# Two attentions rewritten as fp32 products on row tiles of TensorE, with block-diagonal keys, in a one-core transformer kernel

## The chip, the cores and the metric

The kernel runs on one core of one Trainium2 chip. The metric is the time of one execution on the device, in microseconds (us). The kernel before took 394.37 us, the median of three executions (393.59 to 395.58).

## What is computed

1024 rows (16 batches of 64) of 256 features pass through two layers, each with a cross attention and a feed-forward part:

```python
x = x + L0_xattn(layernorm(x), ctx, ctx)      # 32 query heads, 8 key/value heads, 8 features per head
x = x + L0_ffn(layernorm(x))                  # 2 experts 256 -> 1024 -> 256, the better one per row
x = x + L1_xattn(layernorm(x), ctx, Wq, Wkv_expand, Wout)   # 16 heads of 16 features, causal mask
x = x + L1_ffn(layernorm(x))                  # down to 128, 8 experts (top 2 per row) and a shared one, up to 256, plus gelu(x) @ core_w
```

An attention is softmax(q k^T * scale) v within one batch: 64 queries, 64 keys, per head.

## The kernel before

The rows lie in 8 tiles of 128 rows (2 batches each), the feed-forward parts work on 4 groups of two tiles. A tile t goes through the steps of `attn0`, its group through `ffn0`, then `attn1` and `ffn1`. `steps_and_needs` lists the steps and what each needs, `make_orders` is a list scheduler at build time that turns a table of costs (`COST`) and of preferences (`URGENCY`) into one fixed order per engine, and each engine runs its list with semaphores. PSUM has eight banks: four in ring S (attentions and small products), two in H (hidden values of the feed-forward parts), two in Y (their results). A step that fills a bank first claims it, which waits until the bank's former content has been read out.

The names, by step of a tile:

- `attn0`. POOL (`keys0`) and DVE (`queries0`) split fp32 keys and queries into three bfloat16 parts, laid out as 48 of 64 columns (`KS`, `QS`). PE transposes them (`turn_keys0`, `turn_queries0`, against `identb`), ACT and DVE copy them out (`QT`, `K2`). `scores0` multiplies them in bfloat16, four times per tile. DVE takes the row maxima and subtracts them (`scores_less_max0`: `MN`, `PT`), ACT takes the exponential, PE transposes the fp32 probabilities (`turn_probs0`, against `identf`), ACT copies them out, `values0` multiplies by the values `V2`, `turn_back` transposes, DVE divides and adds to `X`.
- `attn1`. `keys_values1` and `project` make keys, values and queries. Both are split into bfloat16 parts (`KQS`), transposed (`turn_heads1`) and copied out (`KT1`, `QT1`). `scores1` gives the scores (causal mask `maskS` by a product with `identb`), DVE takes the maxima (`largest1`), `shifts1` and `turn_shifts1` bring the negated maxima across (`MS1`, `MT1`), and `probs1` forms the transposed scores anew with the shift added by a product with `sel`, so that ACT's exponential is at once the transposed probabilities. `values1` multiplies by the values.
- `ffn0` and `ffn1`: `up0` (H<-XT,WF), `down0` (Y<-WP,A), `up1` (H<-GH,W), `down1` (Y<-A,W), with XN the normalized rows and XT their transposes. `zero_row` (S<-GB,W) works out once what each expert gives for a zero input, one column at a time.

In the trace an fp32 product stands as two records of TensorE, each with a weight load of its own; a bfloat16 product or an fp32 transpose stands as one.

## Time and profile before

| | |
|---|---|
| median of three executions | 394.37 us |
| span of the profiled execution, first to last instruction (its own time; the page has no other) | 397.0 us |
| TensorE busy, records | 366.7 us, 3768 |
| DVE / ACT / POOL busy | 234.5 / 197.6 / 91.7 us |
| granted TensorE clock, mean | 0.957 |
| bytes moved | 12.16 MB, nearly all in the first 40 us |

A record of TensorE lasts some 0.2 to 0.4 us but the next starts before it ends. What a product costs in a dense stream is therefore the distance from its start to the next start, and it is read here from the starts of consecutive groups in the timeline. Granted clock 1.00 is 2.4 GHz, 0.5 is 1.2 GHz.

### The profile page before, as it was taken

What the parts mean: (1) busy time and instruction counts of PE and PEld (TensorE: products, weight loads), DVE (VectorE), ACT (ScalarE), POOL (GpSimd) and SP (SyncE); (2) the same over time, 40 slices, a digit from 0 to 9 for tenths busy, and PEclk for the clock granted to TensorE, in tenths of its full rate; (3) what the DMA queues carried; (4) which work ended last, traced back from release to release, by engine and by line L of the source; (5) the groups of instructions that cost most, each with busy time, mean ns of one, the idle gap of its engine ahead of it and who ended that gap; (6) DMA issues with size and microseconds to landing.
All of it is one profiled execution on the core that took longest, in us unless ns stands there. A gap on an engine that the chain in (4) does not pass through costs nothing.

```text
span 397.0 us, 9308 instructions
## 1 busy us (share of the span) xinstructions
PE 366.7 (92%) x3768; PEld 305.9 (77%) x3768; DVE 234.5 (59%) x611; ACT 197.6 (50%) x403; POOL 91.7 (23%) x173
## 2 busy tenths in 40 slices
PE   1777899999999999999998999999899999997896
PEld 1466888888988888878886877878778787785783
DVE  6689668889997247302399013873756556427134
ACT  1666337567656424232343133656745665666452
POOL 7882113241123223202540312410004000200000
PEclk9988559999999999999999989999989999999899
DMA  9991000000000000000000000000000000000000
GB/s 188 415 390 72 2 1 2 0 3 2 2 0 2 2 0 2 2 3 1 2 2 2 1 3 0 2 2 0 4 28 2 0 2 30 2 1 3 25 0 27
DMA packets 8218, 12.16 MB, mean 31 GB/s; under 512 B 4464, under 2 KB 6768, under 8 KB 7408
## 3 DMA queue, kind: packets, MB, share of 16 engines
q1 hardware_dynamic: 8176, 11.57, 8.7%
q8 instruction: 30, 0.49, 0.5%
q14 instruction: 12, 0.10, 0.1%
HBM read 10.52 MB, written 1.05 MB: 29 GB/s over the span
## 4 chain that ended last, share of the span: by engine, by line
PE 85%; DVE 9%; issue 3%; ACT 2%; POOL 1%; DVEq 0%; POOLq 0%
PE Y L1252 26%; PE H L1252 24%; PE S L1252 20%; PE S L1293 4%; PE S L1353 3%; PE S L1260 2%; PE S L1317 2%; PE S L1269 1%; PE S L1418 1%; DVE PT L1016 1%; DVE MN L1015 1%; PE S L1326 1%; DVE K L1229 0%; DVE KQS L1075 0%; ACT YS L821 0%
## 5 line engine op out<-in xcount | busy, mean ns | idle before, releaser
L1252 PE MATMUL H<-XT,WF 128*128 128x256 f32 x256 | 64.3, 399 | 0.0
L1252 PE MATMUL Y<-WP,A 128*128 128x256 f32 x256 | 59.7, 381 | 0.0
L895 POOL TENSOR_TENSOR A<-R 128x512 f32<-128x512 f32 x32 | 33.4, 1043 | 98.5 <-ACT R L775 96.6
L1252 PEld LDWEIGHTS H<-XT,WF 128*128 128x128 f32 x256 | 49.0, 199 | 8.1 <-ACT R L775 0.8
L1252 PEld LDWEIGHTS Y<-WP,A 128*128 128x128 f32 x256 | 47.5, 190 | 6.0 <-issue 0.2
L803 ACT ACTIVATE A<-H,B 128x256 f32<-128x256 f32 x84 | 35.5, 473 | 28.5 <-PE H L1252 27.0
L775 ACT ACTIVATE R<-H 128x512 f32<-128x512 f32 x32 | 19.1, 597 | 58.5 <-PE H L1252 52.4
L1252 PE MATMUL Y<-A,W 128*128 128x256 f32 x168 | 45.9, 386 | 0.8 <-DVE YG L1206 0.8
L1252 PE MATMUL H<-GH,W 128*128 128x256 f32 x168 | 45.1, 396 | 0.4 <-ACT GH L792 0.4
L1206 DVE TENSOR_TENSOR YG<-YS,Y 128x256 f32<-128x256 f32 x32 | 13.5, 420 | 39.6 <-ACT YS L821 39.2
L1252 PEld LDWEIGHTS H<-GH,W 128*128 128x128 f32 x168 | 31.6, 197 | 6.1 <-issue 1.3
L1252 PEld LDWEIGHTS Y<-A,W 128*128 128x128 f32 x168 | 29.7, 191 | 6.9 <-issue 1.2
L698 ACT COPY QT<-S 128x1024 bf16<-128x1024 bf16 (+1 forms) x24 | 20.3, 885 | 15.0 <-PE S L1260 9.5
L698 ACT COPY QT_OT<-S 96x1024 bf16<-96x1024 bf16 (+1 forms) x32 | 21.0, 692 | 10.7 <-PE S L1252 6.8
L848 POOL TENSOR_TENSOR rstdf<-varef,mhalf 128x2 f32<-128x2 f32 x8 | 5.6, 699 | 89.8 <-DVE varef L971 89.7
L742 ACT ACTIVATE PT<-PT 128x512 f32<-128x512 f32 x32 | 19.6, 629 | 9.0 <-DVE PT L1016 8.9
L1293 PE MATMUL S<-identf,PT 128*128 128x128 f32 x128 | 19.6, 298 | 4.6 <-issue 2.0
L1293 PEld LDWEIGHTS S<-identf,PT 128*128 128x128 f32 x128 | 16.4, 155 | 7.5 <-issue 5.2
L698 ACT COPY PT<-S 128x512 f32<-128x512 f32 x32 | 17.6, 588 | 8.9 <-PE S L1293 8.9
L1089 DVE RECIPROCAL rec<-S 128x16 f32<-128x16 f32 x8 | 2.0, 256 | 33.1 <-PE S L1317 33.0
L821 ACT ACTIVATE YS<-Y,Y0n 128x256 f32<-128x256 f32 x32 | 15.0, 473 | 9.0 <-PE Y L1252 8.5
L1252 PE MATMUL S<-PT,V 64*32 64x64 f32 (+1 forms) x768 | 17.0, 238 | 2.5 <-issue 2.4
(189 smaller groups left out, 659.9 us busy)
## 6 DMA issues: line engine op xcount, KB each, us to landing
W<-in_w SPq DMA_DIRECT2D x2, 1344.0 KB, 11.4
WF<-in_wf SPq DMA_DIRECT2D x2, 1024.0 KB, 7.5
WP<-in_wp SPq DMA_DIRECT2D x2, 1024.0 KB, 9.6
X<-in_x SPq DMA_DIRECT2D x8, 128.0 KB, 8.2
out_dram<-X SPq DMA_DIRECT2D x8, 128.0 KB, 1.7
CD<-in_ctx_in SPq DMA_DIRECT2D x2, 256.0 KB, 5.3
C<-in_ctx_in SPq DMA_DIRECT2D x1, 256.0 KB, 3.0
CT<-in_ctxT SPq DMA_DIRECT2D x1, 256.0 KB, 4.0
```

The source lines that it names most:

```text
L698: nc.scalar.copy(dst(n, i), src(b, i)).then_inc(done, 1)
L742: nc.scalar.activation(e, e, ACT.Exp, scale=HD0 ** -0.5).then_inc(exp_ready, 1)
L775: nc.scalar.activation(R0[:, n % 2, :], b[:, :], ACT.Prelu, alpha=0.5).then_inc(done, 1)
L803: ins = nc.scalar.activation(A1[:, n % 4, :], b[:, k * GT:(k + 1) * GT], ACT.Gelu, bias=B1[:, ch:ch + 1])
L821: nc.scalar.activation(YS[:, j % 2, :], b[:, 0:GT], ACT.Identity, bias=Y0n[:, e:e + 1]).then_inc(ys_ready, 1)
L895: nc.gpsimd.tensor_tensor(flat(A0[:, n % 2, :, :]), R0[:, n % 2, :], R0[:, n % 2, :], ALU.mult).then_inc(a0_ready, 1)
L1206: nc.vector.tensor_tensor(YG[:, j % 2, :], YS[:, j % 2, :], b[:, GT:2 * GT], ALU.mult).then_inc(free["Y", "dve"], 1)
L1252: return nc.tensor.matmul(o, a, b, start=start, stop=stop, skip_group_check=shared)
L1260: ins = nc.tensor.transpose(b[:, :].bitcast(bf16)[:, p * P:(p + 1) * P], flat(QS[:, t % 2, 2 * pair_:2 * pair_ + 2, :]), identb[:, :])
L1293: ins = nc.tensor.transpose(b[:, i * P:(i + 1) * P], PT[:, t % 2, 4 * c + i, :], identf[:, :])
L1317: ins = nc.tensor.transpose(b[:, i * P:(i + 1) * P], o, identf[:, :])
L1353: ins = nc.tensor.transpose(b[:, :].bitcast(bf16)[0:96, h * P:(h + 1) * P], flat(src[:, t % 2, 8 * i + h, :, :]), identb[:, :])
```

## The change

Both attentions are now computed from fp32 queries and keys without the split.

- Keys. A tile's keys are laid out with their features on partitions (`KR0`, loaded so by DMA for layer 0; a product for layer 1) and multiplied by a 0/1 column (`quarter0`, `quarter_`) into four copies, in each of which only one head of a group of four is non-zero (`KZ0` by POOL, `KT1` by DVE). A product of the turned queries (`QT0`, `QT1`, two fp32 transposes or the product itself) with such a block gives the scores of four heads at once.
- `scores0` and `probs0` use 32 rows of the array per product, and each of the four row strips writes a PSUM bank of its own; `scores1`, `probs1` and the layer-0 shift use 64 rows. `values0` and `values1` alternate between two row halves and two banks.
- Layer 0 takes its probabilities as layer 1 did: maxima (`largest0`), turned shifts (`shifts0`, `turn_shifts0`), then a second, transposed score product with the shift added (`probs0`), and the exponential straight from PSUM. `turn_probs0`, the exponential in SBUF and its copy are gone. Layer 1's mask of the transposed scores is now in further rows of `sel` and `MT1`.
- POOL adds the result of layer 0 to `X` (`add_result0`) in DVE's place, and no longer splits keys.
- `zero_rows`: 20 fp32 products whose weights are 8 columns and whose moving side is 128 columns, in place of 20 with 128 and 1.
- `COST`, `URGENCY` (a number per step and tile), `SWITCH`, `CHANGE` and `SLACK` are new, so all orders are new. One line: `"attn0": "c 400.1 -352.5  v -755.8 129.1 ..."` became `"attn0": "c -426 -336 468 727 -863 -12 576 173; v 48 181 ..."`.

```diff
+    if part in ("attn0", "attn1") and stage in "spo":
+        return stages(part, n, {"s": f"h*{SCORE_BANKS[part]}", "p": f"f*{SCORE_BANKS[part]}", "o": "u*2"}[stage])
...
             def keys0(t, _):
                 if t == 0:
-                    pool.wait_ge(ld_c, 16)
+                    pool.wait_ge(places_ready, 1)
...
-                nc.gpsimd.tensor_scalar(KQS[:, t % 2, :, 4, :], rest, 1.0, 0.0, ALU.mult, ALU.add)
-                nc.gpsimd.tensor_tensor(KQS[:, t % 2, :, 2, :], rest, KQS[:, t % 2, :, 1, :], ALU.subtract
-                                        ).then_inc(ks1_ready, 1)
+                    filled(pool, "attn0", t - 2, "f", 3)
+                for c in range(DC):
+                    nc.gpsimd.tensor_tensor(KZ0[:, t % 2, c, :, :], KR0[:, c, t * P:(t + 1) * P].unsqueeze(1).to_broadcast([P, 4, P]),
+                                            quarter0[:, :].unsqueeze(2).to_broadcast([P, 4, P]), ALU.mult).then_inc(kz_ready, 1)
+            def add_result0(t, _):
+                read_out(pool, "attn0", t, "n", 0)
+                for half in range(2):
+                    xh = X[:, t, half * P:(half + 1) * P].rearrange("p (k g r) -> p g k r", k=4, g=2)
+                    o = O0[:, t % 2, half * P:(half + 1) * P].rearrange("p (g k r) -> p g k r", k=4, g=2)
+                    nc.gpsimd.tensor_tensor(xh, xh, o, ALU.add).then_inc(x0_ready, 1)
             def biases(g, _):
...
             def queries0(t, _):
                 wait_rstd("attn0", t)
-                link(normed("attn0", t, 0, t, Q[:, t % 2, :]))
...
-                    filled(dve, "attn0", t - 2, "q", 1)
-                q = Q[:, t % 2, :].rearrange("p (h d) -> p h d", d=HD0)
-                rest = QR[:, t % 2, :].rearrange("p (h d) -> p h d", d=HD0)
-                s = QS[:, t % 2, :, 0:SLOTS * HD0].rearrange("p h (s d) -> p h s d", d=HD0)
-                link(nc.vector.tensor_copy(s[:, :, 0:3, :], q.unsqueeze(2).to_broadcast([P, NH0, 3, HD0])))
-                link(nc.vector.tensor_tensor(rest, q, s[:, :, 0, :], ALU.subtract))
-                link(nc.vector.tensor_copy(s[:, :, 3:5, :], rest.unsqueeze(2).to_broadcast([P, NH0, 2, HD0])))
-                nc.vector.tensor_tensor(s[:, :, 5, :], rest, s[:, :, 3, :], ALU.subtract).then_inc(qs_ready, 1)
-            def blocks0(t, _):
-                b, done = filled(dve, "attn0", t, "k", 0)
-                for half in range(2):
...
+            def largest0(t, c):
+                b, done = filled(dve, "attn0", t, "h", c)
+                nc.vector.tensor_reduce(MN[:, slot("attn0", t), 8 * c:8 * c + 8],
+                                        b[:, :].rearrange("p (h t) -> p h t", t=S), AX.X, ALU.max, negate=True
+                                        ).then_inc(done, 1)
...
             def keys1(t, _):
                 b, done = filled(dve, "attn1", t, "kv", 0)
-                dve.wait_ge(kh_ready, 4 * t + 4)
+                dve.wait_ge(kh_ready, t + 1)
                 if t >= 2:
-                    dve.wait_ge(ks1_ready, t - 1)
-                nc.vector.tensor_tensor(R1[:, t % 2, :].rearrange("p (h d) -> p h d", d=HD1),
-                                        b[:, 0:D].rearrange("p (h d) -> p h d", d=HD1), KQS[:, t % 2, :, 0, :],
-                                        ALU.subtract).then_inc(done, 1)
+                    filled(dve, "attn1", t - 2, "f", 1)
+                nc.vector.tensor_tensor(KT1[:, t % 2, :, :, :].rearrange("p b c k -> p b (c k)"),
+                                        b[:, 0:D].unsqueeze(1).to_broadcast([P, 4, D]),
+                                        quarter_[:, :].unsqueeze(2).to_broadcast([P, 4, D]), ALU.mult).then_inc(done, 1)
             def rows1(t, _):
...
-            def scores0(t, c):
-                b, done = claim(pe, "attn0", t, "s", c)
-                if c == 0:
-                    read_out(pe, "attn0", t, "k", 0)
-                read_out(pe, "attn0", t, "q", c // 2)
-                for i in range(4):
-                    pair_ = 4 * c + i
-                    for bt in range(2):
-                        ins = mm(b[bt * S:(bt + 1) * S, i * P:(i + 1) * P], QT[:, t % 2, pair_, bt * S:(bt + 1) * S],
-                                 flat(K2[:, t % 2, pair_ // 2, bt, :, :]))
-                ins.then_inc(done, 1)
...
+            def scores0(t, _):
+                claims_ = [claim(pe, "attn0", t, "h", i) for i in range(4)]
+                read_out(pe, "attn0", t, "q", 0)
+                pe.wait_ge(kz_ready, 2 * t + 2)
+                for c in range(DC):
+                    for i, (b, done) in enumerate(claims_):
+                        quarter = slice(32 * i, 32 * i + 32)
+                        for bt in range(2):
+                            rows = slice(bt * S, (bt + 1) * S)
+                            ins = mm(b[rows, 4 * c * S:4 * (c + 1) * S], QT0[quarter, t % 2, c, rows], KZ0[quarter, t % 2, c, :, rows])
+                        if c == DC - 1:
+                            ins.then_inc(done, 1)
+            def turn_shifts0(t, _):
+                b, done = claim(pe, "attn0", t, "m", 0)
+                pe.wait_ge(ms0_ready, t + 1)
+                nc.tensor.transpose(b[:, :].bitcast(bf16)[:, 0:P], MS0[:, t % 2, :, :, :].rearrange("p a k h -> p (a k h)"),
+                                    identb[:, :]).then_inc(done, 1)
+            def probs0(t, _):
+                claims_ = [claim(pe, "attn0", t, "f", i) for i in range(4)]
+                read_out(pe, "attn0", t, "m", 0)
+                if t == 0:
+                    pe.wait_ge(sel0_ready, 1)
+                for j in range(8):
+                    for k in range(2):
+                        for r in range(2):
+                            i = 2 * r + k
+                            half = slice(r * S, (r + 1) * S)
+                            for bt in range(2):
+                                rows = slice(bt * S, (bt + 1) * S)
+                                mm(claims_[i][0][rows, j * S:(j + 1) * S], sel0[half, 8 * i + j, :], MT0[half, t % 2, rows],
+                                   start=(j == 0), stop=False, shared=True)
+                for j in range(8):
+                    c, r = divmod(j, 4)
+                    for i, (b, done) in enumerate(claims_):
+                        quarter = slice(32 * i, 32 * i + 32)
+                        for bt in range(2):
+                            rows = slice(bt * S, (bt + 1) * S)
+                            ins = mm(b[rows, j * S:(j + 1) * S], KZ0[quarter, t % 2, c, r, rows], QT0[quarter, t % 2, c, rows],
+                                     start=False, shared=True)
+                        if j == 7:
+                            ins.then_inc(done, 1)
...
             def values0(t, _):
-                b, done = claim(pe, "attn0", t, "o", 0)
+                claims_ = [claim(pe, "attn0", t, "u", bt) for bt in range(2)]
                 pe.wait_ge(v2_ready, 2 * t + 2)
-                read_out(pe, "attn0", t, "p", 3)
-                o = b[:, :].rearrange("p (h g b s) -> p h g b s", h=2, g=2, b=2)
+                read_out(pe, "attn0", t, "f", 3)
                 for kh in range(2):
-                    for bt in range(2):
+                    for part in range(2):
                         for k4 in range(4):
-                            kv = 4 * kh + k4
-                            ins = mm(o[32 * k4:32 * k4 + 32, kh, :, bt, :], flat(V2[:, t % 2, bt, kv, :, :]),
-                                     PT[:, t % 2, 2 * kv:2 * kv + 2, bt * S:(bt + 1) * S])
-                ins.then_inc(done, 1)
+                            first = 8 * k4 + 4 * kh + part
+                            for bt, (b, done) in enumerate(claims_):
+                                rows = slice(bt * S, (bt + 1) * S)
+                                ins = mm(b[32 * k4:32 * k4 + 32, kh * P:(kh + 1) * P], V2[rows, t % 2, 4 * kh + k4, part, :],
+                                         PT[rows, t % 2, first:first + 3:2, :], start=(kh == part == 0), stop=(part == 1), shared=True)
...
+            def scores1(t, _):
+                banks = [claim(pe, "attn1", t, "h", r)[0] for r in range(2)]
+                read_out(pe, "attn1", t, "kv", 0)
+                read_out(pe, "attn1", t, "w", 0)
+                if t == 0:
+                    pe.wait_ge(masks_ready, 3)
+                for b in banks:
                     for bt in range(2):
                         rows = slice(bt * S, (bt + 1) * S)
-                        ins = mm(b[rows, h * S:(h + 1) * S], QT1[:, t % 2, 8 * c + h, rows], KT1[:, t % 2, 8 * c + h, rows],
-                                 start=False, shared=True)
-                ins.then_inc(done, 1)
+                        mm(b[rows, :], identb[:, rows], maskS[:, :].unsqueeze(1).to_broadcast([P, 8, S]), stop=False, shared=True)
+                for c in range(DC):
+                    for r, b in enumerate(banks):
+                        half = slice(r * S, (r + 1) * S)
+                        for bt in range(2):
+                            rows = slice(bt * S, (bt + 1) * S)
+                            ins = mm(b[rows, 4 * c * S:4 * (c + 1) * S], QT1[half, t % 2, c, rows], KT1[half, t % 2, :, c, rows],
+                                     start=False, shared=True)
+                        if c == DC - 1:
+                            ins.then_inc(full["S"], 1)
...
+            def probs1(t, _):
+                banks = [claim(pe, "attn1", t, "f", r)[0] for r in range(2)]
+                read_out(pe, "attn1", t, "m", 0)
+                for j in range(8):
+                    for r, b in enumerate(banks):
+                        for bt in range(2):
+                            rows = slice(bt * S, (bt + 1) * S)
+                            mm(b[rows, j * S:(j + 1) * S], sel[:, 8 * r + j, :], MT1[:, t % 2, rows], start=(j == 0), stop=False,
+                               shared=True)
+                for j in range(8):
+                    c, k = divmod(j, 4)
+                    for r, b in enumerate(banks):
+                        half = slice(r * S, (r + 1) * S)
+                        for bt in range(2):
+                            rows = slice(bt * S, (bt + 1) * S)
+                            ins = mm(b[rows, j * S:(j + 1) * S], KT1[half, t % 2, k, c, rows], QT1[half, t % 2, c, rows],
+                                     start=False, shared=True)
+                        if j == 7:
+                            ins.then_inc(full["S"], 1)
...
+            def values1(t, _):
+                claims_ = [claim(pe, "attn1", t, "u", bt) for bt in range(2)]
+                read_out(pe, "attn1", t, "f", 1)
                 for hq in range(4):
                     for h4 in range(4):
                         h = 4 * hq + h4
-                        ins = mm(b[32 * h4:32 * h4 + 32, hq * S:(hq + 1) * S], V1[rows, t % 2, h, :], PT1[rows, t % 2, h, :])
-                ins.then_inc(done, 1)
+                        place = 8 * (hq % 2) + 4 * (hq // 2) + h4
+                        for bt, (b, done) in enumerate(claims_):
+                            rows = slice(bt * S, (bt + 1) * S)
+                            ins = mm(b[32 * h4:32 * h4 + 32, hq * S:(hq + 1) * S], V1[rows, t % 2, h, :], PT1[rows, t % 2, place, :])
+                            if h == NH1 - 1:
+                                ins.then_inc(done, 1)
             def turn_rows(part):
                 def f(g, _):
...
+            def zero_rows(g, _):
+                b, done = claim(pe, "ffn1", g, "z", 0)
+                pe.wait_ge(ld_w2, 16)
+                pe.wait_ge(gb8_ready, 1)
+                for ch in range(NCH1 - 1):
+                    ins = mm(b[0:E1, 0:L], GB8[:, ch, :], W2[:, ch, :], start=(ch == 0), stop=(ch == NCH1 - 2))
                 ins.then_inc(done, 1)
```

The order of TensorE at the start of the program, last rows up to the first product of a feed-forward part (H<-XT,WF); before:

```order
L1260 MATMUL S<-identb,QS 128x128 x16
L1252 MATMUL S<-GB,W 128x1 x13
L1418 MATMUL S<-identf,XN 128x128 x4
L1252 MATMUL S<-GB,W 128x1 x7
L1252 MATMUL S<-WR,XT 128x2 x4
L1252 MATMUL S<-K,QT 64x128 x16
L1252 MATMUL H<-XT,WF 128x256 x4
```

and after:

```order
L1243 MATMUL S<-QT,KZ 64x64 x64
L1269 MATMUL S<-identb,MS 128x128
L1243 MATMUL S<-MT,sel 64x64 x64
L1243 MATMUL S<-QT,KZ 64x64 x64
L1243 MATMUL S<-PT,V 32x128 x64
L1321 MATMUL S<-identf,OT 128x128 x4
L1249 MATMUL S<-identf,Q 128x128 x4
L1321 MATMUL S<-identf,OT 128x128 x4
L1243 MATMUL S<-KZ,QT 64x256 x16
L1429 MATMUL S<-identf,XN 128x128 x4
L1243 MATMUL S<-WR,XT 128x2 x4
L1243 MATMUL H<-XT,WF 128x256 x4
```

The split transposes (QS, KS, KQS) and half of the PT transposes that stood ahead of this place are gone; in their stead stand the shift and score products of two tiles (MT,sel and QT,KZ) and the zero-input rows have moved behind it.

TensorE at the transposed scores and the values of layer 1 for tiles 0 and 1, before:

```order
L1252 MATMUL S<-maskT,identb 64x512 x2
L1252 MATMUL S<-MT,sel 64x64 x16
L1252 MATMUL S<-QT_OT,KT 64x64 x16
L1252 MATMUL Y<-WP,A 128x256 x8
L1252 MATMUL S<-maskT,identb 64x512 x2
L1252 MATMUL S<-MT,sel 64x64 x16
L1252 MATMUL S<-QT_OT,KT 64x64 x16
```

and after (MT,sel and QT,KT are one step for all 16 heads of a tile now):

```order
L1243 MATMUL S<-MT,sel 64x64 x32
L1243 MATMUL S<-QT,KT 64x64 x32
L1243 MATMUL S<-MT,sel 64x64 x32
L1243 MATMUL S<-QT,KT 64x64 x32
L1321 MATMUL S<-identf,OT 128x128 x4
L1243 MATMUL H<-XT,WF 128x256 x4
L1243 MATMUL S<-PT,V 32x64 x64
L1243 MATMUL Y<-WP,A 128x256 x4
```

The mask product is gone, a tile's 64 products follow one another, and a feed-forward block stands between them and the values.

## Rows read from the trace of the kernel before

**Rows 1.** The page: span, busy time, slices and the chain.

```profile
span 397.0 us, 9308 instructions
...
PE 366.7 (92%) x3768; PEld 305.9 (77%) x3768; DVE 234.5 (59%) x611; ACT 197.6 (50%) x403; POOL 91.7 (23%) x173
...
PEclk9988559999999999999999989999989999999899
...
PE 85%; DVE 9%; issue 3%; ACT 2%; POOL 1%; DVEq 0%; POOLq 0%
```

**Rows 2.** Busy time of each engine in two stretches.

```profile
0.00:54.90 54.90, 38.65 (x385) 32.86 (x385) 41.03 (x96) 25.27 (x46) 29.42 (x82) 0.81 0.58 193
54.90:397.00 342.10, 328.06 (x3386) 273.05 (x3384) 193.50 (x516) 172.38 (x357) 62.30 (x91) 0.98 0.02 5
```

**Rows 3.** TensorE's timeline: start us, length, group, its records.

```profile
8.04 1.06 PE L1269 MATMUL S<-identb,KS 128*64 128x128 bf16 x16 [8.04 <-POOL KS L869]
...
54.88 3.48 PE L1252 MATMUL H<-XT,WF 128*128 128x256 f32 x8
```

**Rows 4.** TensorE's timeline through steps of layer-0 attention.

```profile
105.11 1.51 PE L1293 MATMUL S<-identf,PT 128*128 128x128 f32 x12
106.46 1.06 PE L1260 MATMUL S<-identb,QS 128*128 128x128 bf16 x16
107.44 0.64 PE L1269 MATMUL S<-identb,KS 128*64 128x128 bf16 x16
108.01 1.08 PE L1252 MATMUL S<-PT,V 128*32 128x128 f32 x32
109.02 0.41 PE L1252 MATMUL S<-K,QT 128*64 128x128 bf16 x8
109.37 2.00 PE L1252 MATMUL H<-XT,WF 128*128 128x256 f32 x8
```

**Rows 5.** TensorE's timeline through steps of layer-1 attention.

```profile
304.80 1.06 PE L1353 MATMUL S<-identb,KQS 128*96 128x128 bf16 x16
305.69 0.65 PE L1252 MATMUL Y<-A,W 128*128 128x256 f32 x2
...
326.77 0.41 PE L1252 MATMUL S<-maskT,identb 128*64 128x512 bf16 x2
327.02 0.42 PE L1252 MATMUL S<-MT,sel 128*64 128x64 bf16 x16
327.26 0.42 PE L1252 MATMUL S<-QT_OT,KT 96*64 96x64 bf16 x16
327.52 0.39 PE L1252 MATMUL S<-maskT,identb 128*64 128x512 bf16 x2
...
334.83 0.99 PE L1252 MATMUL S<-PT,V 64*32 64x64 f32 x64
335.76 0.29 PE L1468 MATMUL S<-identb,GS 128*128 128x128 bf16 x2
```

**Rows 6.** TensorE's timeline of 334.83 to 334.86 us alone.

```profile
334.83 0.26 PE L1252 MATMUL S<-PT,V 64*32 64x64 f32 x4
```

**Rows 7.** TensorE's timeline behind a burst, and the instruction DMA of 228.5 to 229 us.

```profile
228.74 1.51 PE L1252 MATMUL S<-PT,V 64*32 64x64 f32 x101
231.18 0.63 PE L1252 MATMUL S<-PT,V 64*32 64x64 f32 x27 [0.92 <-issue]
...
232.44 3.37 PE L1252 MATMUL H<-XT,WF 128*128 128x256 f32 x8
...
q8 instruction: 1, 0.02, 13.5%
```

**Rows 8.** Groups of instructions by line: busy us, mean ns, idle before.

```profile
L1022 DVE TENSOR_REDUCE MN<-S 128x8 f32<-128x512 f32 x16 | 10.4, 686 | 4.5 <-PE S L1252 4.4
L746 ACT ACTIVATE PT<-S 128x512 f32<-128x512 f32 x16 | 9.3, 596 | 11.1 <-PE S L1252 10.2
L895 POOL TENSOR_TENSOR A<-R 128x512 f32<-128x512 f32 x32 | 33.4, 1043 | 98.5 <-ACT R L775 96.6
```

525 lines of the change are left out of this document (225 added, 300 removed), and 33 rows, old and new, of the table URGENCY.

## The prediction, made before the changed kernel had run

> **What bounds the kernel now.** I read the page first. TensorE is busy for 366.7 of 397.0 us and the chain that ended last runs through it for 85% of the span [rows 1]. The other engines are busy for 59%, 50% and 23%. Then the two stretches: behind the first feed-forward product TensorE is busy for 328.1 of 342.1 us at a granted clock of 0.98. Ahead of it, 54.9 us pass with 38.7 us of records at 0.81 [rows 2]. That product starts at 54.88 us, the first record of all at 8.04 [rows 3]. So there are two accounts: the dense stream, where every us of TensorE's work counts, and the start, where the first tiles run through all engines one after the other.
>
> **Prices in the dense stream**, from start to start. An fp32 transpose of 128 columns: 12 in 1.35 us, 0.1125 us each. I take that as the price of an fp32 record by itself: 0.1125 us per 128 moving columns. On column tiles records overlap: 32 records of 128 columns on 32-wide tiles took 1.01 us in place of 3.6 [rows 4], and 64 records of 64 columns took 0.93 us in place of 3.6 [rows 5], so four tiles give close to four times. No row shows two different row strips of the array at work. I take it that they overlap like the columns, which makes the price of a record alone over the number of tiles in use (8 in layer 0 and in both value steps, 4 in layer 1's scores). Its bounds are that (full overlap) and the price on columns alone (none).
>
> **Layer 0, a tile.** Removed or replaced: 16 PT transposes 1.80 us, 16 QS 0.98, 16 KS 0.57, values 1.01, 32 score products at 8 in 0.35 us 1.4 [rows 4]. That is 5.76 us, of which the score figure holds a mode switch too often (some 0.2), so 5.56. Added: 2 transposes 0.23. Scores, 16 products, 32 records of 256 columns: 32 x 0.225 / 8 = 0.90. Shift transpose 0.06. Shift products, 64 in bfloat16 of 64 columns: those of before go at 16 in 0.24 us on two column tiles [rows 5], 15 ns each, so 0.48 on four tiles and 0.96 on two; I take 0.70. Transposed scores, 128 records of 64 columns: 128 x 0.056 / 8 = 0.90. Values, 64 records of 128 columns on 8 tiles: 0.90. Three mode switches more, about 0.1 each, 0.3. Sum 4.0. Saved: 1.55 us a tile, 12.4 us in all.
>
> **Layer 1, a tile.** Removed or replaced: 32 KQS transposes at 16 in 0.89 us, 1.78. Two score steps at 0.26, 0.52 (their mask stays). Two transposed steps of 0.25 mask, 0.24 shift and 0.26 scores, 1.50. Values 0.93 [rows 5]. Sum 4.73. Added: scores, 16 records of 256 columns on 4 tiles, 16 x 0.225 / 4 = 0.90. Shift, 32 at 15 ns, 0.48. Transposed scores, 64 x 0.056 / 4 = 0.90. Values 64 x 0.056 / 8 = 0.45. Two switches 0.2. Sum 2.93. The query and key projections stream as many columns as before: nothing. Saved 1.8 us a tile, 14.4 us in all. The zero-input rows cost 40 records either way (between -4 and +1 us, taken as nothing). **Dense account: 27 us less.** The product counts of the new order give 5105 records against 3768.
>
> **The start.** Ahead of the first feed-forward product the order of before has some 24 us of work at the dense prices, the new one 12.7 (8 fp32 transposes, scores of three tiles, two key products, shift, transposed scores and values of two tiles, 8 transposes back, XN and the router). So 31 of the 54.9 us were loss. The new chain: first queries at 6 us, POOL's key blocks two passes of 1.04 us a tile [rows 8], so scores at 7 to 8.7 on the slow clock. Then 4 maxima of 0.69, shift 0.4, transposed scores 3 us with their supply stall, 4 exponentials of 0.60 [rows 8], and the second tile behind the same banks until 24.5. Values, turn back, division, POOL's addition, layer norm and router take until about 34. Bounds 28 and 44. Loss 21 in place of 31: **10 us less**.
>
> **What hides the rest.** DVE loses four subtraction passes a tile, the key-block copies and all splits, and gains two passes' length for `KT1` (a 512-column pass is 0.69 us, so 1.4). ACT loses the copies of the transposes. POOL gains two passes of 1.04 and some 0.9 us of addition a tile and loses its ten split instructions [rows 8]. At 59%, 50% and 23% before [rows 1] none of them comes near TensorE's load, and the feed-forward blocks of 3.5 us are the cover: if they did not stand between scores and maxima, a tile of layer 0 would show 2.7 + 0.7 us of DVE and ACT, and then 2.4 us of exponentials.
>
> **Instruction supply.** Behind a burst of small records TensorE stood still for 0.92 us with nothing to wait for, after 101 of 128 value records. An instruction block of 0.02 MB was fetched at that time [rows 7]. 0.02 MB is 256 instructions, 128 records with their loads. Stepping back 128 records from the restart at 231.18 leads to 228.3, so a block can't be used up faster than in 2.9 us. I walked both orders in blocks of 128 records at the dense prices. Before, three or four places are faster than that (0.5 to 1.3 us each, 3.7 in all). After, with 192 records per transposed layer-0 step, eight places behind the start are, up to 2.0 us each, 11.7 in all. **8 us more**, between 0 and 14. The Trainium skill ("Runtime: NRT & Kernel Launch", section "Instruction fetch mechanics") says that the sequencer fetches the next page while it executes the current one and that crossing a boundary is mostly hidden. By that the sum would be 8 us lower. The 0.92 us of this trace says otherwise.
>
> **Clock.** Behind that stall 8 feed-forward records took 3.37 us against 2.00 [rows 4, 7], as they do at the lower of the two levels (1.2 and 2.4 GHz); such stretches are the 8s in the page's clock row [rows 1]. More stalls may bring two or three more such stretches of 1.4 us each: 3 more, between 0 and 14.
>
> **Sum.** 397.0 - 27 - 10 + 8 + 3 = 371 us of span. The median of before is 2.6 us below the profiled span, so I predict **368 us**.
>
> **Rivals.**
> 1. Row strips don't overlap (the slower side). Then only columns do, and layer 0's scores and transposed scores cost 3.6 us each in place of 0.9 per tile at two column tiles, shifts 0.96, values 1.8. That is 6.6 more a tile, 52 in all. Layer 1's scores, transposed scores and values are 0.9, 0.9 and 0.45 dearer, 18 in all. With the supply stall gone (-8), 368 + 62 = 430 us. It decides from the point where overlap between strips falls under about half: +26 us makes it slower than before. For it: no row shows an overlap of strips. Against it: column tiles overlap fully in fp32, and each strip has its own bank. Chance 0.11. The Trainium skill ("TensorE: Matmul & The Clock Gate", section "Measured speedup vs the span model") gives 3.07 times for four row tiles and 10.6 for sixteen, which would make this rival unlikely. No row here shows it.
> 2. A record has a least distance. The smallest mean distance of rows 5 is 15 ns, and the new steps ask for 7. If 15 held, 1024 + 1024 + 768 + 512 small records would take 3328 x 0.015 = 50 us in place of the 33 above: 385 us. Against it: four value records started inside 30 ns [rows 6]. Chance 0.10. The skill's same page (section "Wait — 56ns, not 53.3ns?") puts the least start-to-start distance at about 25 ns. By that the sum would be 50 us higher, near 418. Rows 5 and 6 contradict it, and of the 0.10 I give it 0.02.
> 3. Four banks at once. A layer-0 score or probability step claims all of ring S. If TensorE finds no feed-forward work meanwhile, 3.4 + 2.4 us a tile lie bare: 46 us for all eight, 23 for half, about 391, no change. Before, TensorE hardly waited behind the start [rows 2]. Chance 0.08.
> 4. The supply and the clock cost nothing, and the start ends at 28: 368 - 8 - 3 - 6 = 351. Chance 0.10.
>
> The forecast itself, 358 to 380, has 0.61.
>
> **Range and chances.** Rivals 2 and 4 and the forecast lie between 350 and 392, with part of rival 3: 8 in 10. Under 0.5% (2 us) a difference can't be told from none. Faster 0.83, same 0.04 (a strip overlap or bank waits that just eat the gain), slower 0.13 (rival 1, and the worse part of 3).
>
> **What the profile after would show.** Right: layer-0 score groups of 64x256 products, 32 records within a us; QT,KZ with 128 records in 0.9 to 1.2 us apart from stalls; stalls put down to issue of up to 2 us in the steps MT,sel, QT,KZ or PT,V; first H<-XT,WF near 34 us; DVE's busy time down to about 165 us, TensorE's share of the chain above 85%. Wrong: 32 score records over 3 us (strips in turn); QT,KZ evenly 15 ns apart; TensorE waiting for DVE's maxima or ACT's exponentials in mid-program; granted clock under 0.93.

## The result, and the profile after

The changed kernel takes 390.31 us (median of 7; 387.58 to 392.79) against 394.37 (median of 7). The ratio is 0.989, with a 95% interval of 0.9856 to 0.9925. It is faster by about 1%, where 7% (368 us) was forecast, and 390 lies just inside the upper end of the range. The profiled execution has a span of 387.8 us; 371 was forecast.

The page after. Its rows answer to [rows 1]:

```profile
span 387.8 us, 11733 instructions
...
PE 345.8 (89%) x5105; PEld 282.2 (73%) x5105; DVE 163.6 (42%) x481; ACT 150.4 (39%) x349; POOL 90.8 (23%) x134
...
PEclk9999969989999999899999999999999999999899
...
PE 82%; issue 6%; DVE 4%; SPq 3%; ACT 3%; POOL 1%; DMA 1%; DVEq 0%; POOLq 0%
```

TensorE has 5105 records, as counted, and 21 us less busy time. But the chain now holds two names that it lacked before, SPq (SP issuing DMAs, 3%) and DMA (1%), and twice the share of issue. The two stretches, cut at the new place of the first feed-forward product, answer to [rows 2]:

```profile
0.00:53.20 53.20, 26.00 (x650) 19.43 (x651) 22.79 (x57) 12.90 (x31) 26.61 (x54) 0.96 0.60 209
53.20:388.00 334.80, 319.79 (x4456) 262.75 (x4456) 140.84 (x424) 137.48 (x318) 64.23 (x80) 0.98 0.02 5
```

This settles where to look. Behind the first feed-forward product the forecast was 371 - 34 = 337 us; it took 334.6 (387.8 - 53.23), against 342.1 before. The start was to fall from 54.88 to 34 us and fell to 53.23: **19 us late, a little more than the whole miss**. Inside those 53 us TensorE's records fell from 38.7 to 26.0 us, so its work shrank as forecast, and waiting took its place: TensorE stood for 27.2 us. The clock of 0.96 can't be set beside the 0.81 of [rows 2]. The profile counts a stretch for which it has no clock record as full speed, and its first record here lies at 42.55 us (at 16.97 in the kernel before, so that 0.81 is too high as well). Steps ahead of it take up to twice their later time (tile 0's scores 1.94 us against 1.05), as they would at the lower level. TensorE's timeline through the start (start, length, group, idle before it and what ended it; of the scores of tiles 0 and 1, which stand in groups of 4 records, only the first group):

```profile
7.69 0.70 PE L1243 MATMUL H<-KZ,QT 32*64 32x256 f32 x4 [1.99 <-POOL KZ L882]
...
16.94 1.22 PE L1243 MATMUL S<-CT,WKV 64*128 64x128 f32 x4 [6.62 <-DMA WKV<-in_wkv]
...
23.54 1.07 PE L1243 MATMUL S<-MT,sel 64*64 64x64 bf16 x64 [0.66 <-ACT MT L718]
24.54 1.51 PE L1243 MATMUL S<-QT,KZ 32*64 32x64 f32 x74
29.91 1.21 PE L1243 MATMUL S<-QT,KZ 32*64 32x64 f32 x54 [3.86 <-issue]
...
36.18 2.20 PE L1243 MATMUL S<-QT,KZ 32*64 32x64 f32 x121 [1.28 <-issue]
39.42 0.65 PE L1243 MATMUL S<-PT,V 64*32 64x128 f32 x6 [1.04 <-ACT PT L766]
...
53.23 3.22 PE L1243 MATMUL H<-XT,WF 128*128 128x256 f32 x7
```

Two things strike. TensorE stands 6.62 us for layer 1's key and value weights, which its order has ahead of tile 1's scores and the shift of tile 0. And the first burst of short records stands 3.86 us for nothing but its own instructions; the longest such stall of before was 2.0 us. SP's queue says why the weights are late (issue time, length, count):

```profile
1.18 2.67 SPq L679 DMA_DIRECT2D KR<-in_ctxT  x4
...
4.51 2.53 SPq L679 DMA_DIRECT2D KR<-in_ctxT  x4
...
8.81 2.55 SPq L679 DMA_DIRECT2D KR<-in_ctxT  x4
11.41 0.60 SPq L689 DMA_DIRECT2D CT<-in_ctxT  x1
12.05 0.60 SPq L690 DMA_DIRECT2D WKV<-in_wkv  x1
```

An issue costs SP some 0.6 us here, for 32 KB (KR, the first eight) as for 256 KB (CT), and the replicated keys are 12 issues, 7.75 us. In the kernel before WKV was issued at 2.83 us.

### The profile page after: what moved, and what is told of

It reads as the page before. It is cut to its first block, busy times and chain, and to the rows that moved or that the text cites. A ratio compares the mean times of both kernels' runs of the same rounds, so it can differ in the third digit from the quotient of the medians.

```text
span 387.8 us, 11733 instructions
## 1 busy us (share of the span) xinstructions
PE 345.8 (89%) x5105; PEld 282.2 (73%) x5105; DVE 163.6 (42%) x481; ACT 150.4 (39%) x349; POOL 90.8 (23%) x134
## 3 DMA queue, kind: packets, MB, share of 16 engines
HBM read 11.04 MB, written 1.05 MB: 31 GB/s over the span
## 4 chain that ended last, share of the span: by engine, by line
PE 82%; issue 6%; DVE 4%; SPq 3%; ACT 3%; POOL 1%; DMA 1%; DVEq 0%; POOLq 0%
PE Y L1243 27%; PE S L1243 27%; PE H L1243 24%; SPq L679 2%; PE S L1321 2%; DMA WKV<-in_wkv 1%; ACT PT L766 1%; PE S L1429 1%; PE S L1330 1%; POOL X L891 1%; SPq L674 1%; DVE XN L1002 0%; DVE MN L1030 0%; ACT YS L842 0%; PE S L1249 0%
## 5 line engine op out<-in xcount | busy, mean ns | idle before, releaser
L1243 PE MATMUL Y<-WP,A 128*128 128x256 f32 x256 | 64.0, 399 | 0.0
L1243 PE MATMUL H<-XT,WF 128*128 128x256 f32 x256 | 62.1, 391 | 0.0
L1243 PEld LDWEIGHTS Y<-WP,A 128*128 128x128 f32 x256 | 48.9, 199 | 8.1 <-issue 1.5
L1243 PEld LDWEIGHTS H<-XT,WF 128*128 128x128 f32 x256 | 47.9, 194 | 7.9 <-issue 1.5
L766 ACT ACTIVATE PT<-S 128x512 f32<-128x512 f32 x32 | 16.7, 602 | 30.1 <-PE S L1243 30.1
L1243 PE MATMUL S<-QT,KZ 32*64 32x64 f32 x1024 | 15.8, 255 | 10.2 <-issue 10.2
L882 POOL TENSOR_TENSOR KZ<-KR,quarter 128x512 f32<-128x512 f32 x16 | 16.3, 1039 | 33.8 <-PE S L1243 32.0
L1243 PEld LDWEIGHTS S<-QT,KZ 32*64 32x64 f32 x1024 | 13.8, 149 | 11.3 <-issue 10.9
L1046 DVE TENSOR_REDUCE MN<-S 128x8 f32<-128x512 f32 x16 | 10.4, 685 | 22.5 <-PE S L1243 22.5
L1014 DVE TENSOR_SCALAR Q<-X,mv,rstd 128x256 f32<-128x256 f32 x8 | 4.1, 516 | 34.2 <-POOL rstd L869 15.8
L1030 DVE TENSOR_REDUCE MN<-S 128x8 f32<-128x512 f32 x24 | 15.1, 680 | 6.6 <-PE S L1243 6.6
```

The lines of the kernel that those rows point to most:

```text
L766: nc.scalar.activation(flat(PT[:, t % 2, 8 * c:8 * c + 8, :]), b[:, :], ACT.Exp, scale=HD0 ** -0.5).then_inc(done, 1)
L882: nc.gpsimd.tensor_tensor(KZ0[:, t % 2, c, :, :], KR0[:, c, t * P:(t + 1) * P].unsqueeze(1).to_broadcast([P, 4, P]), quarter0[:, :].unsque ...
L1030: nc.vector.tensor_reduce(MN[:, slot("attn0", t), 8 * c:8 * c + 8], b[:, :].rearrange("p (h t) -> p h t", t=S), AX.X, ALU.max, negate=True ...
L1046: nc.vector.tensor_reduce(MN[:, slot("attn1", t), 8 * c:8 * c + 8], b[:, :].rearrange("p (h t) -> p h t", t=S), AX.X, ALU.max, negate=True ...
L1243: return nc.tensor.matmul(o, a, b, start=start, stop=stop, skip_group_check=shared)
```

## Experiments

Theory 1: SP's queue makes the start late. Theory 2: the instruction supply sets it. Theory 3: the chain through DVE and ACT sets it. Theory 4 came after the first runs: the supply is slow because data loads fill the DMA engines. Ratios are to the kernel before, which ran again beside each group of runs (medians 394.4 to 395.9 us), each with its 95% interval. The changed kernel stands at 0.989 (0.986 to 0.993), with its first feed-forward product at 53.23 us. "First product" means that one from here on; times inside a run are from its one trace.

### Three ways to have WKV early

WKV first:

```diff
             keys(0, 0, 1)
+            sp.dma_start(CT[:, :], ctxT).then_inc(ld_kv, 16)
+            sp.dma_start(WKV1[:, :], wkv1).then_inc(ld_kv, 16)
             rows(1)
```

> The two loads that layer 1's key and value step needs (CT, WKV) are issued behind the first tile's rows and keys, 12 issues earlier; nothing else changes. Theory 1 (SP's queue of issues makes the start late): WKV is issued near 4.5 us in place of 12.05 and has landed near 9.5, so the wait of 6.62 us for it goes, the first feed-forward product comes 5 to 7 us earlier than 53.23, and the time falls by 5 to 7 us, to 384. Theory 2 (the stalls of TensorE's instruction supply set the start, and the wait is hidden under them): under 1.5 us gained. Theory 3 (DVE's maxima and ACT's exponentials set the start): under 2 us gained, and the wait for WKV turns into waits for GS, MS or PT of the same length.

Measured: 388.01 us, ratio 0.983 (0.977 to 0.988), span 384.8, first product at 49.38. The wait for WKV is gone and the first shift products start 5.0 us earlier. Only 3.9 of these reach the first product. A third stall has grown from 0.35 to 1.99 us. The ratio's interval overlaps that of the changed kernel, so it is the trace that shows the gain, and not the time:

```profile
24.30 1.20 PE L1243 MATMUL S<-QT,KZ 32*64 32x64 f32 x54 [3.28 <-issue]
...
30.57 2.19 PE L1243 MATMUL S<-QT,KZ 32*64 32x64 f32 x121 [1.28 <-issue]
...
36.44 3.64 PE L1243 MATMUL S<-PT,V 64*32 64x128 f32 x122 [1.99 <-issue]
```

Keys in 6 issues in place of 12 (a source access with a broadcast dimension):

```diff
-                for r in range(4):
-                    sp.dma_start(KR0[r:P:4, :, ...], rows_of[:, :, ...])
+                for c in range(DC):
+                    sp.dma_start(KR0[:, c, ...], ctxT[32 * c:32 * c + 32, ...].unsqueeze(1).to_broadcast([32, 4, ...]))
```

> The replicated keys KR are loaded with one DMA per 32 rows of the transposed context (6 issues on SP in place of 12), the same bytes. Theory 1: WKV is 13th in the queue in place of 19th, issued near 8.3 us in place of 12.05, and the first feed-forward product and the end come 3 to 4 us earlier (387). A rival within it (the transfers themselves are late, not their issues): WKV lands at 16.9 as it does now and the time stays. Theories 2 and 3: under 1.5 us.

Measured: 387.15 us, ratio 0.982 (0.978 to 0.986), span 384.8, first product at 51.58. WKV is issued 4.1 us earlier, at 7.97, but its products start only 1.4 us earlier, at 15.55. The rest is lost in the transfer, beside data that is moved earlier too, so the rival within theory 1 holds for most of it.

Eight key loads from ACT's queue:

```diff
+            for k in range(2):          # scalar block, first thing
+                for r in range(4):
+                    act.dma_start(KR0[r:P:4, :, k * P:(k + 1) * P], ...)
```

> 8 of the 12 key loads go out on ACT's queue, which has nothing else to do in the first 5 us; SP issues rows of tiles 0 and 1, CT, WKV and then the rest. Theory 1: WKV is issued near 2.8 us and hidden, tile 1's rows come 2 us earlier too, the first feed-forward product comes 8 to 10 us earlier (44 to 45), time 381. If ACT's own issues delay its first copies or the first keys, some 2 us of this are lost. Theories 2 and 3: under 2 us gained.

Measured: 386.28 us, ratio 0.978 (0.973 to 0.983), span 385.1, first product at 48.60. The reason that was named for a smaller gain explains 1.9 us of it: ACT's issues delay its first copy, so tile 0's scores start at 9.61 in place of 7.69, "3.81 <-ACT QT". The other 1.7 to 2.7 us that are missing from the forecast (44 to 45) aren't explained. So WKV's place is worth 1.7 to 4.6 us of the 19 at the first product, and not its 6.6. Theory 3 falls as the main cause at this stage: of the waits for DVE and ACT only the one for tile 1's Q appeared behind WKV first (1.61 us, tile 1's rows being issued 1.2 us later).

### The order alone

Layer 1's key and value step of tiles 0 and 1 behind tile 2's scores, on all three engines:

```diff
         orders = make_orders()
+        for t in (1, 0):
+            move("pe", ("attn1", t, "kv", 0), ("attn0", 2, "s", 0))
+            move("act", ("attn1", t, "kv", 0), ("attn0", 3, "q", 0))
+            move("dve", ("attn1", t, "kv", 0), ("attn0", 2, "h", 3))
```

> Only the order: layer 1's key and value products of tiles 0 and 1 go on TensorE behind the scores of tile 2 (on ACT behind the queries of tile 3, on DVE behind the maxima of tile 2), where TensorE now waits 2.40 us for XN; the loads stay as they are. Theory 1, second half (what stands ahead of m0 in TensorE's order delays the whole start, wait and 3.7 us of products alike): p0 starts near 14 in place of 23.54, the first feed-forward product comes 7 to 10 us earlier than 53.23, time 381 to 383. Rival (instruction blocks come at a fixed pace of about 6 us each while the data loads run, whatever the order): p0 starts early but its stall grows, and under 5 us are gained, as in the run with WKV's load first.

Measured: 392.00 us, ratio 0.989 (0.984 to 0.994): nothing gained. This is the run that refuted the plain reading of the 6.62 us. The shift products start at 15.53, 8 us earlier, and then:

```profile
22.04 1.01 PE L1254 MATMUL S<-QT,KZ 32*64 32x64 f32 x41 [3.82 <-issue]
...
31.55 2.01 PE L1254 MATMUL S<-QT,KZ 32*64 32x64 f32 x108 [4.41 <-issue]
...
37.71 3.23 PE L1254 MATMUL S<-PT,V 64*32 64x128 f32 x109 [2.15 <-issue]
```

The three stalls come to 10.4 us in place of 5.5, which takes 4.9 of the 8. Behind the values (40.94) the run is 2.5 us ahead of the changed kernel. The moved step takes the rest: it now stands at 46.97 to 50.9, with two waits of its own for DVE, 1.43 and 0.75 us, where the 2.40 us for XN are saved, and the first product comes at 54.40. The restarts lie 9.5 and 6.2 us apart. [rows 7] gave 2.9 us as the least for a block. So the rival's outcome holds (the stalls grow, under 5 us gained), but not its fixed pace of 6 us.

### The loads held back

On the kernel with WKV first, SP waits before the weights:

```diff
+            read_out(sp, "attn0", 1, "f", 3)
             sp.dma_start(WR0[:, :, :], wr0).then_inc(ld_f0, 16)
```

> On the kernel with WKV's load first: SP waits for the last exponential of tile 1 before it issues the loads from WR on (5 MB), so that the first two transposed score steps run with no data load beside them. Theory 4 (an instruction block is fetched late while the queues are full of data: there restart follows restart by 5.7 to 6.3 us, against about 2.9 behind the loads): the stalls of 3.28, 1.28 and 1.99 us shrink to 1.5 us together, the first feed-forward product comes at 45 in place of 49.38, the time falls by 4 us to 384. Rival (the stall is a matter of TensorE's own sequencer, loads don't matter): stalls as before, and the time the same, or longer by what WF and WP then are late.

Measured: 391.03 us, ratio 0.984 (0.978 to 0.990), first product at 52.69. The stalls did as theory 4 says: 1.09 us in place of 3.28, and none in place of 1.28 and 1.99. Tile 2's scores start at 36.60 in place of 42.77. Then TensorE waits 11.47 us for XN, because DVE stands behind tile 4's rows, whose load had been held too. One line of the profile names the cure:

```profile
45.55 0.43 DVE L993 BATCH_NORM_STATS2 stats<-X 128x6 f32<-128x256 f32 x1 [9.31 <-DMA X<-in_x]
```

With the rows of tiles 4 to 7 issued ahead of the wait (two lines moved):

> As the run with held loads, but the rows of tiles 4 to 7 are issued before SP waits, so that only the weights are held. There DVE stood 9.31 us for tile 4's rows, which its order has ahead of the first feed-forward's layer norm, and gave back all that the shorter stalls had gained. Theory 4: stalls in the first tiles 1.1 us as there, XN waits 2.4 us again, the first feed-forward product starts near 43.3 in place of 49.38, time 382. Rival (WR and WF, issued near 30 us, now set the start): the wait moves to them, first product not before 46, time 386.

Measured: **381.57 us, ratio 0.966 (0.962 to 0.971)**, span 380.1, first product at 44.64. It computes the same as the changed kernel with the same instructions but one wait; only SP's order differs. The gain is all in the start. Behind the first product the stalls for issue came to 7.8 us in place of 6.1.

```profile
21.34 1.21 PE L1244 MATMUL S<-QT,KZ 32*64 32x64 f32 x54 [1.21 <-issue]
...
25.84 2.26 PE L1244 MATMUL S<-QT,KZ 32*64 32x64 f32 x128
29.15 2.25 PE L1244 MATMUL S<-PT,V 64*32 64x128 f32 x128 [1.04 <-ACT PT L767]
...
42.94 1.84 PE L1244 MATMUL S<-WR,XT 128*128 128x2 f32 x8 [3.10 <-DMA WF<-in_wf]
```

Both sides were right in part: 3.10 us now go to WF, issued too late. The fetches themselves can be seen. In the changed kernel, 23.6 to 27.4 us, all packets are data (q1) while the burst runs and then waits; the block comes at 27.4 to 28.7:

```profile
q1 hardware_dynamic: 639, 1.49, 100.9%
```

```profile
q8 instruction: 1, 0.02, 5.5%
```

With the weights held, the same block comes in the stretch 18.6 to 19.9 us, which begins one us after the burst's start at 17.62:

```profile
q8 instruction: 1, 0.02, 5.9%
```

So the block is started late (about 4 us behind the burst's start against 1). Its transfer is over within a stretch of 1.3 us either way. The other traces say the same: from the first shift product to the packet it is 3.5 to 4.0 us in the five runs with loads under way (3.95 in the changed kernel, 3.49 with WKV first, 3.93 with the order alone), and 0.95 and 1.00 us in the two with loads held. From the packet to TensorE's restart it is 2.3 to 2.7 us in all of them. The Trainium skill ("DMA: Bandwidth & Descriptors", section "Queues, rings and completion order") says that a DMA engine alternates between the rows it has work for, a packet at a time. By that a block would hardly wait behind data. These traces have it starting 3 us later, and no run here shows what holds it up before its transfer.

### The number of records

Shift products of layer 0 left out:

> Layer 0's 64 shift products of each tile (MT,sel) are left out, so its exponentials are taken without the row's maximum; everything else stands. The products take 0.64 us a tile, 5.1 in all. Theory of the instruction supply (a block of 256 instructions can't be used up faster than in about 2.9 us, and bursts of 192 short records run into it): the step has 128 records in place of 192, and half of the 10.2 us that QT,KZ now waits for issue go as well, so 8 to 11 us faster (380). Rival (the stalls belong to places or to data loads, not to the number of short records): 5 us faster, and QT,KZ still waits about 10 us for issue.

Measured: 375.00 us, ratio 0.949 (0.945 to 0.953), span 373.5. That is 14.3 us of span for 5.1 us of work. Issue waits fell from 11.6 to 5.4 us, and the mean clock rose from 0.977 to 0.986, worth some 3 us more (an estimate: 0.9% of the span). To tell work from records, the same shifts in 8 wide products, with nothing left out:

```diff
-                for j in range(8):
-                    for k in range(2):
...
-                                mm(claims_[i][0][rows, j * S:(j + 1) * S], sel0[half, 8 * i + j, :], MT0[half, t % 2, rows], ...)
+                for bt in range(2):
+                    for k in range(2):
+                        for r in range(2):
+                            i = 2 * r + k
+                            mm(claims_[i][0][rows, :], sel0[half, i, :], W0[half, t % 2, :, rows], stop=False, shared=True)
+            def wide0(t, _):    # DVE, in place of ACT's copy of the shifts
+                nc.vector.tensor_tensor(W0[:, t % 2, :, :], b[...].unsqueeze(1).to_broadcast([P, 8, P]),
+                                        eighth0[:, :].unsqueeze(2).to_broadcast([P, 8, P]), ALU.mult)
```

> Layer 0's shift goes in as 8 products of 512 columns per tile in place of 64 of 64 columns: DVE spreads the transposed shifts over a bank's 8 heads (one pass of 1024 columns from PSUM in place of ACT's copy, about 1.2 us a tile). TensorE's own work falls by 0.2 us a tile, 2 us in all; DVE gains 8 us. Theory of the instruction supply (the number of records in a burst makes the stalls): 448 records fewer, stalls as in the run without shift products (5.4 us in place of 11.6), time 378 to 382. Rival (what helped there was the work left out): 387 to 389, and in the start DVE's pass costs 1 us a tile.

Measured: 383.89 us, ratio 0.969 (0.964 to 0.974), span 382.9. The products cost almost what the 64 did, and the step behind them runs through:

```profile
74.46 0.63 PE L1265 MATMUL S<-W,sel 64*64 64x512 bf16 x8
75.02 1.60 PE L1265 MATMUL S<-QT,KZ 32*64 32x64 f32 x128
```

0.56 us a tile in place of 0.64: half a us of work in all. Behind the first product (54.37) the run is 6.1 us shorter than the changed kernel, 328.5 against 334.6. Issue waits there are 1.8 us in place of 6.1, and the mean clock of the whole run is 0.987 in place of 0.977. So fewer records made most of those 6 us, and the half us of work next to nothing. The places at which one block ends and the next begins moved with the records, and no run moves them alone. The time lies 2 us above the forecast of 378 to 382. The start got 1.1 us longer: the wait ahead of the first shift grew from 0.66 to 3.73 us, because DVE's own pass (1.23 us) now stands ahead of its two for layer 1's KT, and the stalls for issue stayed (2.37, 2.77 and 0.26 us there, against 5.5 in the changed kernel).

### Do row strips overlap, and what sets a record's price

The strip as the outer loop in both steps:

```diff
-                for c in range(DC):
-                    for i, (b, done) in enumerate(claims_):
+                for i, (b, done) in enumerate(claims_):
+                    for c in range(DC):
```

> Layer 0's scores and transposed scores are issued strip by strip: the records that follow one another share their 32 rows of the array and differ only in the two column tiles. Theory (records of different row strips overlap only when they are issued in turn): a score step takes 3.6 us in place of 1.1 (32 x 0.225 / 2), a transposed one 3.6 in place of 1.6 to 2.2, 30 to 36 us more less 5 of stalls: 415 to 420. Rival (TensorE takes strips out of order, or the overlap is between column tiles alone): no change, 390.

Measured: 398.84 us, ratio 1.006 (1.002 to 1.010), span 396.0. A transposed step takes what the theory says, a score step doesn't:

```profile
68.85 3.43 PE L1243 MATMUL S<-QT,KZ 32*64 32x64 f32 x128
78.56 3.88 PE L1243 MATMUL S<-QT,KZ 32*64 32x64 f32 x128
93.48 1.16 PE L1243 MATMUL S<-KZ,QT 32*64 32x256 f32 x32
```

Strips overlap: issued in turn, the 128 records take 1.6 us, strip after strip 3.4 to 3.9. The rival (no change) is refuted by a factor of two in this step. Busy time of these records rises from 15.8 to 34.1 us, issue waits fall from 11.6 to 2.7, and the sum, 9.4, is about the 8.2 us of span. The score step, with 8 records in a strip before the next, lost nothing, which takes 20 us (8 x 2.5) from the forecast of 415 to 420. Why it lost nothing is open.

Then half the columns in each transposed record:

```diff
-                            ins = mm(b[rows, j * S:(j + 1) * S], KZ0[...], QT0[quarter, t % 2, c, rows], ...)
+                            ins = mm(b[rows, j * S:j * S + 32], KZ0[...], QT0[quarter, t % 2, c, bt * S:bt * S + 32], ...)
```

> Every transposed score product of layer 0 (QT,KZ) moves 32 columns in place of 64, so that half of the transposed scores are left out; the number of records stays at 128 a tile. After the change such a step takes 1.53 us for its records, 12 ns each, where 7 ns were forecast from columns over tiles. If columns set the pace, a step takes about half, 0.8 us; if each record has a least distance of its own (rival 2 of the prediction in a milder form), it stays near 1.5 us.

Measured in its trace (one execution, 395.93 us, not used as a comparison):

```profile
68.13 1.49 PE L1243 MATMUL S<-QT,KZ 32*64 32x32 f32 x128
```

1.49 us with 32 columns, 1.59 with 64; from start to next start 1.42 and 1.53, which is 11 and 12 ns a record. So the record sets the price, and not its moving columns. Each record still loads 64 columns of weights in both kernels, and no run here tells that load from the rest of the record.

### Together

The wide shifts with the keys in 6 issues and CT, WKV ahead of tile 1's keys; then the same with rows 4 to 7 issued early, the weights held and WF ahead of WP.

> The kernel with 8 wide shift products, with the keys loaded by 6 DMAs and CT, WKV ahead of tile 1's keys. If the two causes are apart from one another (late WKV in the start, number of records in the dense part), their gains add: the waits of 7.1 us for WKV and 3.7 us for DVE's KT go to under 2 us together, the first feed-forward product starts near 47 in place of 54.37, time 377 to 379. Rival (the stalls of the supply take the gain back, as in the run with the later key and value step): 382 or more.

> The same, and SP issues the rows of tiles 4 to 7, waits for the last exponential of tile 1, and then issues the weights, WF ahead of WP. Theory 4: with no load beside the first tiles the stalls for issue in the start fall under 1 us together, the first feed-forward product starts near 41, time 371 to 374. Rival (weights late): a wait for WF or WP of 3 us and more at 40 to 46 us, 376 or more.

Measured: 377.71 us, ratio 0.957 (0.953 to 0.961), first product at 47.05; and **372.97 us, ratio 0.945 (0.942 to 0.948)**, span 369.9, first product at 43.23. The gains add: in the first of the two the first product comes 7.3 us earlier than with wide shifts alone, and the stretch behind it is as long (328.5 us). The wait of 3.73 us for KT, which was to go, stayed in both. In the second, TensorE's waits for issue ahead of products into S come to 1.3 us against 11.6 (one more, 1.0 us, stands ahead of a product into Y), and the first product waits for no weight:

```profile
PE S L1268 <- issue: 1.3, 4, 0.5
```

```profile
19.32 1.07 PE L1268 MATMUL S<-W,sel 64*64 64x512 bf16 x8 [3.73 <-DVE KT L1102]
...
43.23 3.76 PE L1268 MATMUL H<-XT,WF 128*128 128x256 f32 x8
```

This version beats both kernels: 5.5% below the kernel before, 4.4% below the changed one.

## Why the prediction was wrong

**The failed step is the start.** The prediction said "10 us less", "Loss 21 in place of 31", with the first feed-forward product at "about 34. Bounds 28 and 44". It came at 53.23, 9 us beyond the upper bound. Along its own chain, the first shifts came 11.5 us late (23.54 for 12). The stretch from there to the end of both tiles' exponentials (39.42 for 24.5) took 3.4 us more than forecast, and the rest 4.3 us more. Four things went wrong in it:

1. **It followed the tile and not the queue.** "First queries at 6 us ... so scores at 7 to 8.7" came true (5.04 and 7.69), and maxima were to lead to the first shifts at 8.7 + 2.8 + 0.4 = 12 us. They started at 23.54. Ahead of them in TensorE's order stood the key and value products (the prediction counts them as work and not as a wait) and tile 1's scores, and ahead of their weights in SP's queue stood the 12 new key issues, 7.75 us. SP's queue was never walked; the edit's own DMAs are part of its cost. With WKV early, the shifts started at 18.52 in one run; with only the order changed, at 15.53.
2. **It took one supply price for all times.** 2.9 us a block, from [rows 7], is a price without data loads. In the start restart followed restart by 6.3 and 4.2 us, and by up to 9.5 in the run with the order changed. The prediction had "3 us with their supply stall" for the first transposed step; it took 7.6. Weights held back gave 4.7 and 3.8 us back (49.38 to 44.64, and 47.05 to 43.23), the first of them in spite of 3.10 us for WF. This also swallowed more than half of what moving a step could have given.
3. **It took the slow clock for the first scores alone.** The values of both tiles took 3.92 us from start to next start (0.35 of it a stall) where 1.8 was forecast. In mid-program, at a granted clock of 1.00 on record, they took 2.04:

```profile
84.92 2.11 PE L1243 MATMUL S<-PT,V 64*32 64x128 f32 x128
```

The other steps of the start were longer too, and all stand ahead of 42.55 us, the first record of the clock. My estimate from such distances is 6 us: 0.9 for tile 1's scores, 1.6 for the key and value products, 0.7 for the shifts, 1.4 for the transposed scores, 1.5 for the values. With the weights held, full speed is on record from 28.31 us on, and the values took 2.25. No run changed the clock alone.

4. **It left out the small waits**: 1.5 and 1.04 us for the exponentials, 1.22 for the division, 2.40 for XN. With three shorter ones TensorE's waits for ACT and DVE behind the first scores come to 8.1 us. In the last run, with its first product at 43.23, TensorE's waits for DVE in the start come to 9.9 us behind the first queries (3.73 for KT, 1.82 for the wide shift, 1.22, 2.41 and 0.72). A part of the first two is the wide shift's own pass. So the chain through DVE (theory 3) is most of what idles there, and no run shortened it. The last 9 of the 19 us (43.23 to 34) were not tested one by one.

**Instruction supply**: "8 us more" was 7.2 (11.6 against 4.4 of before), the right sum from the wrong places. "Eight places behind the start ... 11.7 in all" were five, 6.1 us. The rest, 5.5 us, lay in the start. The run with wide shifts bears the mechanism out: nearly the same work in fewer records takes most of the stalls behind the start away. **Clock**: a stall in mid-stream is followed by half speed here too. Behind the 1.58 us at 74.6 the 8 feed-forward records took 3.68 us at a granted clock of 0.51, the lower level as in [rows 7], against 1.99 at full speed:

```profile
76.19 0.50 PE L1243 MATMUL S<-QT,KZ 32*64 32x64 f32 x33 [1.58 <-issue]
76.63 3.68 PE L1243 MATMUL Y<-WP,A 128*128 128x256 f32 x8
```

**Dense account**: right, 334.6 against 337, but by errors that cancel. These rows are one tile's steps in mid-program, to set beside [rows 4, 5]:

```profile
56.60 1.12 PE L1243 MATMUL S<-KZ,QT 32*64 32x256 f32 x32
57.65 3.72 PE L1243 MATMUL H<-XT,WF 128*128 128x256 f32 x16
...
64.86 0.71 PE L1243 MATMUL S<-MT,sel 64*64 64x64 bf16 x64
65.50 1.59 PE L1243 MATMUL S<-QT,KZ 32*64 32x64 f32 x128
67.03 1.99 PE L1243 MATMUL Y<-WP,A 128*128 128x256 f32 x8
```

Layer 0's four steps took 1.05, 0.64, 1.53 and 1.02 us (values of two tiles in 2.04) for 0.90, 0.70, 0.90 and 0.90. Layer 1's took 1.02, 0.63, 1.09 and 0.79 for 0.90, 0.48, 0.90 and 0.45. For six tiles of layer 0 and eight of layer 1 that is 11.4 us dearer. Against it stand 5.6 us of stalls that didn't come, the 3 for the clock (0.98 before and after), and 4 for mode switches, which the distances already held. That is 12.6 against 11.4, where 2.4 are to be explained; the last us is open.

**The rivals.** 1 (strips don't overlap): refuted; 32 records in 1.05 us, where they would take 7.2 one by one (0.225 each). The Trainium skill's page "TensorE: Matmul & The Clock Gate" (section "Measured speedup vs the span model") has products on different row tiles overlap, 3.07 times for four of them. The trace agrees that they do, with 6.9 times on eight tiles (four strips by two column tiles). 2 (a least distance of 15 ns): true in kind, and layer 0's transposed and layer 1's value step pay for it, but at 12 ns (10 in bfloat16); the 1.53 us lie above the 0.9 to 1.2 that the prediction named as a sign of being right. By its own working that is 3328 x 0.012 = 40 us in place of 33, 7 of its 17. The 25 ns of the Trainium skill's same page (section "Wait — 56ns, not 53.3ns?") are contradicted once more. 3 (four banks at once): not seen; behind the start TensorE waits for DVE's maxima 0.8 us in all. 4 (supply and clock cost nothing, start at 28 us): nothing of it came. DVE's busy time (163.6 for 165) was right; TensorE's share of the chain was 82% where over 85 was expected.

## What to carry to other kernels

A change that saves work on TensorE and adds transfers must be walked through the issuing queue too: count 0.4 to 0.7 us for each DMA ahead of the one that is waited for (0.6 in this queue), and order loads by the first wait on them. Bursts of short matmuls wait longer for their instruction blocks while data loads run (3.28 us against 1.09); keep large loads that nobody needs yet away from such bursts, and write one wide product in place of eight narrow ones even where its own time is the same. When a wait is taken away, ask what paces the stretch next: of 8 us won at 15.53 us, 2.5 were left at 40.94 and none at the first product. And check the speed of the start by the length of steps that you know, for the clock row reads full where it has no record.

## What was not expected of the hardware

- Under full data load an instruction block started 3.5 to 4.0 us behind the burst that wanted it (five runs), against 1 us without (two). TensorE went on 2.3 to 2.7 us behind the block's start either way. Restarts in the start were 4.2 to 9.5 us apart.
- fp32 records of 32x64 on eight tiles start 12 ns apart with 64 moving columns (1.53 us for 128) and 11 with 32 (1.42).
- Issuing strip by strip costs the records of 64 columns a factor of 2.2 (15.8 to 34.1 us busy) and those of 256 columns nothing (1.12 to 1.16 us a step).
- SP's issue took 0.6 us for 32 KB and for 256 KB alike, and 0.43 for the 1 MB of WF. Some later ones took over 2 us (2.11 for the 0.5 KB of DB), and no run shows why.
